# A convolution and feed-forward block on one core: the feed-forward part for all tokens, or for the chosen half gathered by indirect DMA

## The reference, cut to what matters

```python
x = x + conv_ref(ln_c(x), ...)     # sign, 3x3 convolution with signed weights, batch norm over all images, relu
t = to_tokens(x)                   # per image 3136 tokens of 128 channels
t = t + ffn_ref(ln_t(t), ...)
def ffn_ref(x, ...):
    weights = x @ wr + br                        # one router weight per token
    idx = top_k(weights, 1568)[:, :1567]         # the 1567 largest of an image's 3136
    sel = x[idx]
    y = gelu(sel @ w1 + b1) @ w2 + b2            # 128 -> 512 -> 128
    y = y * weights[idx]
    return zeros.at[idx].set(y) + x
```

## Time and profile before

| | us |
|---|---|
| median of 3 runs | 2376.41 (2373.12 to 2378.39) |
| the profiled execution | 2379.78 |
| span of its profile, first to last instruction | 2377.8 |
| PE, PEld, DVE, ACT, POOL busy in the span | 2202.0, 1071.6, 1622.5, 1222.9, 918.5 |

### The profile page before, as it was taken

One profiled execution on the slowest core, in us unless ns is written; L12 is line 12 of the kernel. 1 busy time (PEld: TensorE's weight loads), 2 busy tenths in 40 slices (PEclk: granted clock), 3 DMA queues, 4 the chain that ended last, 5 costly groups with the idle time before them and its releaser, 6 DMA issues. The chain is left out here.

```text
span 2377.8 us, 38759 instructions
## 1 busy us (share of the span) xinstructions
PE 2202.0 (93%) x9739; PEld 1071.6 (45%) x9739; DVE 1622.5 (68%) x4887; ACT 1222.9 (51%) x2030; POOL 918.5 (39%) x714
## 2 busy tenths in 40 slices
PE   6999999966999999999999999998999999999997
PEld 3555555533444444444444444444444444444443
DVE  6777777755677766767676666666667676767764
ACT  4444444434555555555555555555555555555553
POOL 1000000024455544445445555454544454554433
PEclk9999999987999999999999999999999999999998
DMA  3444444431122222222222222222222222222201
GB/s 146 163 162 162 162 162 162 162 122 46 62 73 73 74 81 76 81 85 75 73 73 73 73 73 72 73 73 73 81 82 91 73 73 73 73 73 84 73 33 59
DMA packets 66710, 216.99 MB, mean 91 GB/s; under 512 B 28496, under 2 KB 33328, under 8 KB 62640
## 3 DMA queue, kind: packets, MB, share of 16 engines
q1 hardware_dynamic: 66464, 215.71, 25.1%
q10 hardware_dynamic: 144, 0.30, 0.0%
HBM read 136.70 MB, written 77.47 MB: 90 GB/s over the span
## 5 line engine op out<-in xcount | busy, mean ns | idle before, releaser
L950 PE MATMUL ps<-hs,w_c 128*128 128x448 f32 x1792 | 806.9, 564 | 0.8 <-ACT yo L505 0.6
L495 ACT ACTIVATE hs<-ps,b1c,undo 128x448 f32<-128x448 f32 x896 | 602.6, 718 | 136.6 <-PE ps L941 136.0
L412 POOL TENSOR_TENSOR tl<-tr,th 128x448 f16<-128x448 f32 x224 | 245.5, 1096 | 515.7 <-ACT th L518 393.9
L854 PE MATMUL ps<-yo,cwT 128*128 128x448 bf16 x2016 | 425.6, 356 | 0.0
L950 PEld LDWEIGHTS ps<-hs,w_c 128*128 128x128 f32 x1792 | 305.3, 192 | 191.7 <-issue 152.3
L505 ACT ACTIVATE yo<-ps,cols 128x448 f32<-128x448 f32 x224 | 141.9, 633 | 453.6 <-PE ps L950 453.6
L407 POOL TENSOR_TENSOR xb<-xb,zr 128x448 f32<-128x448 f32 x224 | 259.1, 1159 | 182.7 <-ACT zr L511 181.8
L419 POOL TENSOR_TENSOR yo<-yo,base 128x448 f32<-128x448 f32 x224 | 264.5, 1181 | 167.4 <-DVE yo L781 166.6
L939 PE MATMUL ps<-th,w_h 128*128 128x448 f16 x896 | 321.4, 359 | 0.0
L941 PE MATMUL ps<-th,w_l 128*128 128x448 f16 x896 | 319.3, 356 | 0.0
L940 PE MATMUL ps<-tl,w_h 128*128 128x448 f16 x896 | 319.2, 356 | 0.0
(11 more groups left out here) (131 smaller groups left out, 2709.7 us busy)
## 6 DMA issues: line engine op xcount, KB each, us to landing
xb<-x SPq DMA_DIRECT2D x31, 1568.0 KB, 7.6
xb<-x SPq DMA_DIRECT2D x33, 896.0 KB, 4.7
result<-yo SPq DMA_DIRECT2D x32, 896.0 KB, 4.4
y_int<-y SPq DMA_DIRECT2D x32, 784.0 KB, 3.7
xb<-x SPq DMA_DIRECT2D x33, 672.0 KB, 4.3
result<-yo SPq DMA_DIRECT2D x32, 672.0 KB, 3.4
y<-y_int SPq DMA_DIRECT2D x32, 448.0 KB, 5.3
y<-y_int SPq DMA_DIRECT2D x32, 336.0 KB, 4.8
```

Of the source, the lines that this page charges most:

```text
L412: nc.gpsimd.tensor_tensor(cut(tl, c), tr[(b + c) % 2][:, :], cut(th, c), ALU.subtract).then_inc(tl_ready, 1)
L495: nc.scalar.activation(hs[(b + slot) % 2][:, j, :], ps[:, H_BANK + j, 0:T], ACT.Gelu_apprx_tanh, bias=b1c[:, j:j + 1], scale=undo[:, 1:2]) ...
L854: last = M(bank, cwT[:, t, :], sg[b][:, c * ROWS + dy:c * ROWS + dy + ROWS, dx:dx + SIDE], start=t == 0, stop=t == TAPS - 1)
L950: last = M(bank, w2_c[:, j, :], hs[(b + c) % 2][:, j, :], start=first, stop=final)
```

## The change

The convolution stays. Phase 2 now has `POS` = 32 positions per image, and an image passes from position -8 to 137, so six images are in work at once. Tokens are taken strided: tile t holds the tokens 28p + t, p = 0 to 111.

1. `turn_and_dot`: each of 28 tiles is transposed, and its router product is an f32 matmul of the same strided tile with the one column `wr`. All 7 groups share one PSUM bank (`T_BANK`), and begin after all 7 residual additions of the image.
2. `derive` makes scale, mean and router weight per token; `turn` transposes the 28 tiles again, and `token_base` (28 DVE instructions) writes t + ln_t(t) as token rows of 132 f32 (128 values, two numbers with which the row can be normed, the weight, a zero). SP writes the rows to DRAM.
3. The search is as before. New: every chosen token gets a rank, and a list of 1568 row numbers in 14 columns of 112 is built on the chip (`rank_rows`, `difference`, `place`, `index`).
4. POOL issues 14 indirect gathers per image (112 rows of 528 bytes each), DVE norms them (`normalise`), PE transposes them, and hidden, gelu and output run over 1568 tokens in groups of 4, 4, 4 and 2 tiles. The result is transposed back, ACT multiplies it by the weight (`gate_rows`), and POOL issues 14 indirect scatters that add into the rows in DRAM.
5. SP reads all rows back, PE transposes 28 tiles (`turn_back`), ACT writes them to the output tile with a stride (`take_out`), SP stores.

Gone are `transposes`, `router`, `rows_of_stats`, `spread_stats`, `spread_gates`, `scale_tokens`, `centre_tokens`, `split_stats`, `apply_gate`, `gates`, `add_base` and POOL's `low_part` (DVE makes the low part now).

```diff
-POS = 2 * NB * NCH
+POS = 32
+LOAD_AT = -8
+RELU_AT = [0, 2, 4, 6, 8, 10, 12]
+P1_AT = [14, 16, 18, 20, 22, 24, 26]
+VAR_AT = 28
+DERIVE_AT = 32
+P2_AT = [33, 35, 37, 39, 41, 43, 45]
+W_AT, WSE_AT, ROWS_AT = 33, 34, 47
+COUNT_AT = [39, 42, 45, 48, 51, 54, 57, 60]
+TIES_AT, TIES_T_AT, COPY_AT, SCAN_AT, RANK_AT, DIFF_AT, DCOPY_AT, PLACE_AT, INDEX_AT = (
+    61, 62, 63, 64, 65, 66, 67, 68, 69)
+GATHER_AT = [70, 73, 76, 79]
+FFN_AT = 80
+SLOT = 2 * NB
+NORM_AT = [FFN_AT + SLOT * g - 4 for g in range(NG)]
+SELT_AT = [FFN_AT + SLOT * g - 3 for g in range(NG)]
+HIDDEN_AT = [FFN_AT + SLOT * g + j for g in range(NG) for j in range(NB)]
+OUTPUT_AT = [FFN_AT + SLOT * g + NB + j for g in range(NG) for j in range(NB)]
+YEV_AT = [FFN_AT + SLOT * (g + 1) for g in range(NG)]
+YT_AT = [FFN_AT + SLOT * (g + 1) + 1 for g in range(NG)]
+YG_AT = [FFN_AT + SLOT * (g + 1) + 2 for g in range(NG)]
+SCATTER_AT = [FFN_AT + SLOT * (g + 1) + 3 for g in range(NG)]
+READ_AT = 118
+FIN_AT = [123, 125, 127, 129, 131, 133, 135]
+STORE_AT = 137
...
+            sp.dma_start(iota_f, consts[0:1, K_END:K_END + RANKS].to_broadcast([TILE, RANKS])).then_inc(iota_in, 16)
+            sp.wait_ge(zero_ready, 1)
+            for n in range(n_img):
+                sp.dma_start(rows_d[n][TOK:RPI, :], zero[:, :]).then_inc(zero_saved, 16)
...
+                    for m, mb, _ in due(READ_AT, *at):
+                        sp.wait_ge(scattered[mb], (m - mb) * ST * 8 + ST * 16)
+                        if has(m - 1):
+                            sp.wait_ge(fin_t, m * NCH)
+                        sp.dma_start(back, rows_d[m][0:TOK, :].rearrange("(p i) w -> p i w", i=NT)
+                                     ).then_inc(back_in, 16)
...
+            def gather(m, b, g):
+                if g == 0:
+                    pool.wait_ge(idx_ready, m + 1)
+                    pool.wait_ge(rows_saved, (m + 1) * 16)
+                    wait_count(pool, scattered[b], (m // 2) * ST * 16)
+                for t in GROUPS[g]:
+                    nc.gpsimd.indirect_dma_start(
+                        sel[b][:, t, :], None, rows_d[m][:, :],
+                        bass.IndirectOffsetOnAxis(ap=idx[b][:, t:t + 1], axis=0)).then_inc(gathered[g], 16)
+
+            def scatter(m, b, g):
+                pool.wait_ge(yg_ready, m * NG + g + 1)
+                for t in GROUPS[g]:
+                    nc.gpsimd.indirect_dma_start(
+                        rows_d[m][:, :], bass.IndirectOffsetOnAxis(ap=idx[b][:, t:t + 1], axis=0),
+                        sel[b][:, t, :], None, compute_op=ALU.add).then_inc(scattered[b], 16)
...
+                    for m, mb, _ in due(VAR_AT, *at):
+                        rstd(m)
+                    for m, mb, c in due(RELU_AT, *at):
                         residual(m, mb, c)
...
+                    for m, mb, g in due(GATHER_AT, *at):
+                        gather(m, mb, g)
+                    for m, mb, g in due(SCATTER_AT, *at):
+                        scatter(m, mb, g)
...
+            def gate_rows(m, b, g):
+                act.wait_ge(y_t, m * NG + g + 1)
+                for i, t in enumerate(GROUPS[g]):
+                    last = nc.scalar.activation(sel[b][:, t, 0:C], ps[0:TILE, S_BANK, i * C:(i + 1) * C], ACT.Copy,
+                                                scale=sel[b][:, t, C + 2:C + 3])
+                last.then_inc(yg_ready, 1)
...
+            def token_base(m, k):
+                dve.wait_ge(p2_done, m * NCH + k + 1)
...
+                for i in range(TPG):
+                    t = k * TPG + i
+                    last = V.tensor_scalar(rows[:, t, 0:C], ps[0:TILE, T_BANK, i * C:(i + 1) * C],
+                                           onepr[:, t:t + 1], mr_c[:, t:t + 1], ALU.mult, ALU.subtract)
+                last.then_inc(p2_taken, 1)
...
+            def tokens(b, t):
+                return xb[b][:, :].rearrange("c (p i) -> c i p", i=NT)[:, t, :]
+
+            def turn_and_dot(m, b, k):
+                if k == 0:
+                    pe.wait_ge(x1_ready, (m + 1) * NCH)
+                    wait_count(pe, derived, m)
+                    wait_count(pe, p2_taken, m * NCH)
+                wait_count(pe, stats_taken, m * NCH + k)
                 for i in range(TPG):
...
+                    t = k * TPG + i
+                    nc.tensor.transpose(ps[0:TILE, T_BANK, i * C:(i + 1) * C], tokens(b, t), ident)
+                    last = M(dot_ps[:, t:t + 1], tokens(b, t), wr_c, start=True, stop=True)
+                last.then_inc(p1_done, 1)
+
+            def turn(m, b, k):
+                if k == 0:
+                    pe.wait_ge(stats_taken, (m + 1) * NCH)
+                wait_count(pe, p2_taken, m * NCH + k)
+                for i in range(TPG):
+                    last = nc.tensor.transpose(ps[0:TILE, T_BANK, i * C:(i + 1) * C], tokens(b, k * TPG + i), ident)
+                last.then_inc(p2_done, 1)
...
+            def place(m):
+                pe.wait_ge(by_row_ready, m + 1)
+                for t in range(ST):
+                    last = M(place_ps[:, t, :], started[:, t * TILE:(t + 1) * TILE], by_row[:, :], start=True, stop=True)
+                last.then_inc(placed, 1)
```

More of the change, by code:

```diff
@@ L89, in block_kernel @@
     w_dram = nc.dram_tensor("w_row", [n_img, TOK], f32).ap()
+    rows_d = [nc.dram_tensor(f"token_rows{n}", [RPI, RW], f32).ap() for n in range(n_img)]
     with ExitStack() as ctx:
@@ L155, in block_kernel @@
[L155 to L163 removed]
+        cwa = rowbuf[:, 0:C * TAPS]
@@ L888, in router @@
-            def router(n, b, c):
-                pe.wait_ge(tl_ready, n * NCH + c + 1)
-                if c == 0 and has(n - 1):
-                    pe.wait_ge(mask_step, (n - 1) * MASK_STEPS + 3)
-                bank = ps[:, T_BANK, 0:T]
-                for i, (w, t) in enumerate(((wsel_h, th), (wsel_h, tl), (wsel_l, th))):
-                    last = M(bank, w[:, C - c:2 * C - c], cut(t, c), start=c == 0 and i == 0,
-                             stop=c == NCH - 1 and i == 2)
-                if c == NCH - 1:
-                    last.then_inc(w_done, 1)
@@ L940, in hidden @@
-                M(bank, w1_h[:, blk], cut(tl, c), start=False, stop=False)
-                M(bank, w1_l[:, blk], cut(th, c), start=False, stop=True).then_inc(h_done, 1)
-            def output(n, b, c, j):
-                g = n * NCH + c
-                if j == 0:
-                    wait_count(pe, y_taken, g)
-                first, final = j == 0, j == NB - 1
-                bank = ps[:, Y_BANK, 0:T]
-                pe.wait_ge(h_ready, g * NB + j + 1)
-                last = M(bank, w2_c[:, j, :], hs[(b + c) % 2][:, j, :], start=first, stop=final)
+                high, low = (t[g % 2][:, 0:wide(g)] for t in (th, tl))
@@ new lines, in hidden, with output @@
+                M(bank, w1_h[:, blk], high, start=True, stop=False)
+                M(bank, w1_h[:, blk], low, start=False, stop=False)
+                M(bank, w1_l[:, blk], high, start=False, stop=True).then_inc(h_done, 1)
+            def output(m, g, j):
+                if j == 0:
+                    wait_count(pe, y_taken, m * NG + g)
+                pe.wait_ge(h_ready, (m * NG + g) * NB + j + 1)
+                last = M(ps[:, Y_BANK, 0:wide(g)], w2_c[:, j, :], hs[g % 2][:, j, 0:wide(g)], start=j == 0,
+                         stop=j == NB - 1)
@@ L975, in phase2, with turn_back @@
+            def turn_back(m, k):
+                if k == 0:
+                    pe.wait_ge(back_in, (m + 1) * 16)
+                wait_count(pe, out_ready, m * NCH + k)
+                for i in range(TPG):
+                    last = nc.tensor.transpose(ps[:, F_BANK, i * TILE:(i + 1) * TILE], back[:, k * TPG + i, 0:C],
+                                               ident[0:TILE, 0:TILE])
+                last.then_inc(fin_t, 1)
             def phase2(n, b):
                 for pos in range(POS):
-                    c, j = divmod(pos, 2 * NB)
@@ L979, in phase2 @@
-                    if j < NB and has(n):
-                        hidden(n, b, c, j)
-                    if j >= NB and c > 0 and has(n):
-                        output(n, b, c - 1, j - NB)
-                    if j >= NB and c == 0 and has(n - 1):
-                        output(n - 1, 1 - b, NCH - 1, j - NB)
-                    at = (n, b, pos)
-                    for m, mb, c in due(TRANSPOSE_AT, 1, *at):
-                        transposes(m, mb, c, n, pos)
-                    for m, mb, c in due(ROUTER_AT, 0, *at):
-                        router(m, mb, c)
```

700 lines of the change are left out of this document (338 added, 362 removed).

## The result

The changed kernel takes **2931.25 us** (median of 4 runs, 2921.14 to 2940.92) against 2376.0 in the same series (2373.12 to 2378.39): a ratio of 1.234, 95% interval 1.228 to 1.239. The direction was forecast and the size was not: 23% slower where 10% was forecast, and outside the range of 2280 to 2860. The profiled execution took 2924.35 with a span of 2922.5 us.

The account below looks back on a forecast made before the run. PE's list bound the kernel (94% busy, 56.0 us an image). Afterwards a chain of 26.5 + 27.0 + 4.6 + 4.8 = 62.9 us a period, with 557 + 31 x 62.9 + 100, led to 2606 us; range 2280 to 2860.

Parts of the forecast that it names:

- The path over VectorE and TensorE: Period without POOL's DMAs: 25.2 us on DVE, 31.9 from position 14 to the variance, 4.8 power; 61.9 us.
- (a): POOL from an image's power to position 14: seven residuals, 8.1 us, and 16 indirect DMAs at 1.15; 26.5 us.
- (d): POOL from position 27 to the period's end: four scatters, 4.6 us, then the power, 4.8 us.
- (c): Positions 14 to 26 on PE, until POOL may scatter: 19.3 us, plus 7.7 for slow strided loads; 27.0 us.
- (b): DVE's work from the power to position 14, 25.2 us, hidden beside POOL's 26.5.
- LDWEIGHTS of the strided tiles: PE's weight loads in `turn_and_dot`: 0.213 us for 112 strided columns, 2.56 us a group, 1.3 more than unstrided.
- The end: Stretch after the last power, search to last store: about 100 us, before 110.
- Rival 1: Strided loads fast and indirect DMAs issued in 1.03 us or less: period 52.8 us, about 2284 us; chance 0.26.
- Rival 2: Strided loads fast, but an indirect DMA issue on POOL at 1.4 us: period 60.2, 2513 us; chance 0.12.
- Rival 3: POOL's queue the whole bound, 1.9 us an issue: period 70.2 to 77.9, 2823 to 3071 us; chance 0.12.
- The prediction's other estimate: Period if POOL were held for the skill page's 1 us per DMA: 3 us under the sum of 62.9.
- Rival 4: Late landing of scatters and rows read back makes PE stand 5 us: period 68, 2765 us; chance 0.08.

Follow-up runs that it names:

- e2: Changed kernel with its indirect scatters and gathers replaced by plain writes and reads of fixed rows issued by SP, none on POOL; 2576.4 us.
- e9: e2 and e4 together: plain fixed-row DMAs by SP and tiles of neighbouring tokens, against the changed kernel; 2485.09 us.
- e12: Changed kernel with the same indirect scatters on POOL writing instead of adding; 2779.5 us.
- e4: Changed kernel with tiles of 112 neighbouring tokens instead of every 28th, output tile written in order; 2861.48 us.
- e8: Changed kernel with 16 unused f16 matmuls on PE in front of its wait for the residual additions; 2934.89 us.
- e13: e4 and e8 together: tiles of neighbouring tokens and the 16 extra matmuls, against the changed kernel; 2823.28 us.
- e10: e3 with only the first group's four scatters issued two positions later, behind the power; 2692.57 us.
- e6: Changed kernel with every scatter issued two positions later, the first group's behind the power; 2899.59 us.
- e7: e3, e4 and e6 together: residuals on VectorE, tiles of neighbouring tokens, scatters two positions later, against the changed kernel; 2786.8 us.
- e5: e3 and e4 together: residuals on VectorE and tiles of neighbouring tokens, against the changed kernel; 2720.34 us.
- e3: Changed kernel with the seven residual additions moved from POOL to VectorE, one position later, all indirect DMAs left on POOL; 2714.15 us.

## Why the prediction was right in direction and wrong in size

**What held.** No engine is full and the queues decide, as the text said: PE 75% of the stretch, idle before `turn_and_dot` with the residual as releaser. The path over VectorE and TensorE was given 61.9 us, and e2, where it is alone, took 60.9. That this is so near is in part luck: the stretch given 31.9 took 30.6 and 31.1, with the loads of its seven groups 0.6 us a group too dear, 4.2 in all, and the rest too cheap by about 3. By that path the change loses whatever POOL's DMAs cost, and by e9 it also loses with loads in order, 58.0 against a break-even of 55.5. The first power was forecast at 557 and came at 552.6.

**The step that failed** is the price of an indirect DMA in (a) and (d), "16 x 1.15" and four more. Eight gathers cost 1.19 each and twelve scatters 1.6: 28.7 us on the chain instead of 23.0. That is 5.7 of the 9.4 us by which the period read above (72.3) exceeds 62.9. The row it was built on was SP's issue, which holds no adding; e12 shows that the adding alone is 0.54 us a piece. In the same step (a) left out POOL's waits for ACT (3.1 us) and the dearer residual after a scatter or a power (1.64, with the gaps 2.0). (c) gave 1.4 back: 25.6 against 27.0. 5.7 + 3.1 + 2.0 - 1.4 = 9.4. Small slips of the sums don't matter beside this: the terms of (b) add to 25.0, not 25.2, and 16.5 at 94% is 17.6, not 17.7.

**The sentence that misled** was that POOL's price doesn't decide once the loads are slow. Two paths of 62.9 and 61.9 looked like a tie. With true prices one is 71.0 and the other 60.9, and 0.1 us more on each of 20 DMAs is 2 us of period as long as POOL's path is the longer one.

**The loads.** LDWEIGHTS of the strided tiles were to take 0.213 us; they took about 0.18, and a tile 0.47 to 0.49 instead of 0.64, a group 1.95 instead of 2.56. That the stride costs was right, its size was too high. At the full clock a strided load behind an idle stretch takes 0.18 us (0.13 in order, e4), less than ACT's time per element makes it, and a whole tile 1.8 times one in order (0.47 against 0.26). The text had left the lower clock at nothing in the sum. It is 0.50 just there, and (c) came out near its forecast by the two errors against each other: loads too dear by 0.6 a group, f16 products and waits between the groups too cheap. e4, e8 and e13 show that stride and clock overlap: 2.1 us, 0.0 and 3.3 together, the first and the last with PE waiting for the rows on top.

**The end.** 100 us forecast, 169.0 measured. 37 of the 69 missing are POOL's DMAs, since e2 ends in 132.3; the forecast had one image's gathers and scatters there, and after the last power POOL still issues 28 gathers and 38 scatters, of more than two images. Of the other 32, the landing of scatters (3.2) and rows (8.7) with PE idle is in the trace. The rest wasn't taken apart.

**The rivals.** Rival 1 is out: an issue under 1.03 us was not to be had even for a gather from start to start (1.24). Its figure for the other path, 52.8, was too low too, as e9's 58.0 has neither cost. Rival 2 had the average price (1.4 against 1.43) and 60.2 us; the 12.1 it lacks to 72.3 are the stretch (c) (25.6 against 19.3), the waits for ACT, the dearer residuals, and 0.7 from the DMAs. Rival 3 named the right mechanism at the wrong price: its lower time, 2823 at 1.9 us an issue, was passed at 1.43 on average, because the slow loads, the waits for ACT, the dearer residuals and the longer end came on top. The Trainium skill (SBUF — State Buffer, SBUF: two separate sides), which the prediction cited there, has POOL's descriptors held off by DVE's two-port operations. The 448 gathers range from 929 to 1171 ns with a median of 933, so hardly one was held off, and the rule doesn't show here. What shows is VectorE held up beside POOL's residual, in `normalise` (2.57 against 1.11 us for four). The prediction's other estimate, from the Trainium skill (DMA: Bandwidth & Descriptors, Specifications), was 3 us a period under the sum. The page's 1 us is a time to the first byte, and the estimate took it as if POOL were held for it. A gather holds POOL 0.94 us, near that, an adding scatter 1.49, and the measurement decides: the estimate was further off than the sum. The time to the first byte itself shows in no run here. Rival 4 doesn't hold for the changed kernel's periods, whose chain has 1% of DMA. It holds at the end, and it comes back as soon as something else gets shorter or the scatters later: DMA has 8% of the chain in e10, 11% in e4, 12% in e13, 13% in e6 and 14% in e7. It was given 0.08 and is the next limit of this kernel.

**What stays open** is the stall of DVE and ACT for which the trace names no releaser, 163 us of waits in 500 in e7 and 86 in e5. No run took it apart. Open too are what the low clock costs as a whole, and how e3's 6.7 us divide between the order, the work taken from POOL and VectorE's faster `normalise`.

## What to carry to other kernels

Halving an engine's work pays only if no chain over the other engines becomes longer than the list that was cut; add up the new chain first, and every DMA that a compute engine issues counts on it with its whole issue time, at each place where something else queues behind it. An indirect DMA that adds is priced apart from one that moves. Rows that are written and read back make a loop of their own, and its landing times become the limit when the queue gets shorter. When two paths come out within a few per cent, the range has to be made from each one's own unknown prices, not from their near tie.

## What the hardware showed that was not expected

- An indirect DMA of 112 rows of 528 bytes holds POOL for 0.94 us, 1.24 from start to start, as a gather and (e12) as a plain scatter; with adding 1.49, and 1.76 to 1.94. Packets per DMA are 32 and 128.
- The instruction on POOL behind an adding scatter starts within it and shows longer: residual 1.64 instead of 1.13 (behind a power too), power 5.35 instead of 4.80 (e2's powers have a mean of 4797 ns). Behind a gather or e12's plain scatter it doesn't: 1.13 and 1.14.
- TensorE turns a strided f32 tile (step 28) in 0.47 us at a granted clock of 1.00 and 0.49 at 0.50; one of neighbouring columns in 0.26 and 0.49. So the stride is free at half the clock.
- The granted clock was 0.50 from 1275 to 1290 us, around PE's wait of 4.8 us and behind it. Matmuls in the wait raised it to 1.00 from 1285 on, but it fell again at 1297.5, and the period stayed.
- VectorE's `normalise` of four tiles took 2.1 to 2.6 us in the three groups from 1240 to 1460 us beside which a residual ran on POOL, and 1.1 to 1.2 in the groups without one. The residual itself showed its usual 1.13.
